# A decoder layer in fp32r: the context's M and U computed for two heads at once, and new places for the late steps

## The chip, the cores and the metric

One core of a Trainium2 chip. The metric is device microseconds of one execution. The engines are TensorE (PE, the matrix engine, whose weight loads are shown as PEld), VectorE (DVE), ScalarE (ACT), GpSimd (POOL) and SyncE (SP, which issues most DMAs). Each engine works through its own list of instructions in order, and waits on semaphores where it needs another's result.

## The reference

A decoder layer on x of 2 x 1024 x 256 with a context of 2 x 77 x 256, 16 heads of 64 in both attentions:

```
x = layernorm(x + self_attention(x))              # causal, rotary positions
x = layernorm(x + cross_attention(x, context))
x = layernorm(x + routed_ffn(x))                  # only the 512 tokens with the highest router value

cross_attention(query, key=value=context):
    q = query @ w_q; k = key @ w_k; v = value @ w_v       # split into heads
    attn = softmax(q @ k.T / 8)
    return (attn @ v) @ w_o
```

## The kernel before

Every large operand stands as a rounded high half and a low half (the difference), and a product is three matmuls: high by high, high by low, low by high. ACT writes the high half, POOL or DVE the low one.

One function, `plan()`, makes a single ordered list of steps, and each engine runs its own part of every step in that order. A step has a due time, counted in score steps, from hand-written tables; the steps are sorted by it. A step is named by a key and numbers, as sc.126 or kt.3. So the tables decide the order on every engine's queue at once, SP's and POOL's too.

*Self-attention.* Sixteen passes, one for a pair of heads and one batch entry (`NSELF`), with nine score steps each: sc.0 to sc.143. In sc, PE computes a block of scores for the two heads of the pair, one on rows 0 to 63 of the array and one on rows 64 to 127, alternating (line 682). Each has its own PSUM bank; ACT takes the exponentials (line 942). mx is a run of matmuls for the row maxima, with reductions on DVE. pv (line 701) is the product with V, four to a pass. su adds the exponentials, on POOL and some on DVE (line 504). sm sums over keys (line 713), den and nrm turn and spread the reciprocals, op is a piece of the output projection. Of the next passes pj, vp and st are projected and rounded in between.

*The context.* Instead of K and V of the context, the kernel makes for each head M = w_q k' (so that the scores are x times M) and U = v w_o (so that the output is a sum of P times U). For each pair p of heads, eight in all:

- xw.p.0 and xw.p.1: the pair's weights. SP has loaded them into one of two buffers (`load_xw`, line 1621); ACT rounds them, POOL makes the low half (lines 888 and 1451), and SP issues the load of the next pair's half when POOL is done.
- kt.p: `context_kv`, twelve matmuls with 128 rows for keys and values of both heads; ACT and DVE write their halves `XKH`, `XKL`.
- mh.h: `head_m`, M of one head, six matmuls on the 64 rows of that head. ACT copies it out in two pieces (line 1006), DVE makes three low pieces (lines 1278 and 1282).
- uh.h: `head_u`, U of one head, six matmuls of 77 by 256 on the same 64 rows. ACT copies it out, and SP stores it to `ud` in HBM (`keep_u`, line 1671).
- ug.k: U comes back from `ud` in another layout, ten pieces: load (line 1637), ACT, POOL. The load of ug.k+2 waits until POOL is done with ug.k (two buffers). wg are the same for the weights of the feed-forward part.
- tx.2.k turns x for the cross-attention.

PE takes PSUM banks from rings: kt, mh, uh, mx, sm, den, nrm, op and pj share five banks ("self"), taken in turn; `take` waits until the bank's last user has been copied out.

All these steps, keyed by `ENDS`, fall into the last two passes, from sc.126 on. Of pair p, xw, kt, mh and uh come at a fixed offset from `kt + by * p`.

*The rest.* sx.u (scores, 16 tiles of 128 queries), the maxima and exponentials, dn.u (sums on DVE, division on POOL), tp.u (turns) and pu.u (times U); keyed by `TAIL`. lns and lnr are the two halves of a layer norm: statistics on DVE and roots on POOL (line 1499), and rows scaled on DVE (line 1259). lw, lg, ct, sl, ps, id, gt route the tokens, xg turns the chosen ones. h1, fin, fl are the feed-forward part, keyed by `FFN`, and po (`put_rows`, line 1575) scatters the finished rows to the output.

## Time and profile before

| | us |
|---|---|
| median of 3 runs | 923.16 (920.53 to 923.82) |
| the profiled execution | 924.77 |
| its span, first to last instruction | 922.9 |
| PE busy in it | 839.0 (91%) |
| DVE busy | 698.5 (76%) |
| POOL busy | 650.0 (70%) |
| ACT busy | 446.0 (48%) |
| mean granted clock of PE | 0.959 |

Busy time is the union of an engine's instructions. An engine can be busy for all of a stretch and still not be what sets it, so the table of stretches is read together with what each wait names. [...] In PE's timeline matmuls overlap: one starts before the one ahead of it has ended, and the time from start to start is its real cost.

### The profile page before, as it was taken

The numbers are of one execution on the slowest core, as the hardware profiler recorded it, in microseconds if no ns is written. First come the engines' busy times: TensorE is split into PE (matmuls) and PEld (weight loads), VectorE is DVE, ScalarE is ACT, GpSimd is POOL, SyncE is SP. The second block draws the span as 40 slices with busy tenths as digits, with TensorE's granted clock in tenths as the row PEclk, the third lists the DMA queues.
The fourth block names the chain that finished last, engine by engine and source line by source line (L and its number), as shares of the span: only waits on it lengthen the run. The fifth ranks groups of instructions, "written<-read, shape, count | busy, mean of one in ns | idle before, by whom it ended". The sixth has DMA issues, their size and how long they took to land.

```text
span 922.9 us, 17631 instructions
## 1 busy us (share of the span) xinstructions
PE 839.0 (91%) x6322; PEld 625.5 (68%) x6322; DVE 698.5 (76%) x1722; ACT 446.0 (48%) x1009; POOL 650.0 (70%) x636
## 2 busy tenths in 40 slices
PE   2677999999998999999999999999998989878794
PEld 2554666766666667666666676677668979777594
DVE  3678777877879878788898797553359888998674
ACT  2323445455355453553544534655665754553450
POOL 2538697887977979889889898667566432453576
PEclk9879999999999999999999999999999989888798
DMA  8010000000001000000000010333111000120012
GB/s 267 24 58 12 8 24 8 18 25 7 19 1 30 14 7 30 13 8 25 11 14 1 8 36 1 94 90 93 55 44 34 24 24 25 43 71 24 23 47 91
DMA packets 33206, 33.47 MB, mean 36 GB/s; under 512 B 3616, under 2 KB 28000, under 8 KB 33120
## 3 DMA queue, kind: packets, MB, share of 16 engines
q1 hardware_dynamic: 32352, 30.26, 10.8%
q0 software_dynamic: 768, 2.10, 0.7%
q8 instruction: 50, 0.82, 0.4%
q14 instruction: 36, 0.29, 0.1%
HBM read 24.45 MB, written 7.77 MB: 35 GB/s over the span
## 4 chain that ended last, share of the span: by engine, by line
PE 69%; DVE 12%; POOL 6%; issue 6%; ACT 4%; DMA 1%; SPq 1%; DVEq 0%; POOLq 0%; ACTq 0%
PE bank L609 28%; PE bank L682 15%; PE bank L701 13%; PE bank L649 5%; PE bank L614 3%; ACT W_f L1048 2%; PE bank L713 2%; POOL SUM L504 1%; DVE X L1259 1%; DVE W_f L1366 1%; DVE DR L1366 1%; PE bank L687 1%; POOL out L1575 1%; POOL rs L1499 1%; POOL REG L1451 1%
## 5 line engine op out<-in xcount | busy, mean ns | idle before, releaser
L504 POOL TENSOR_TENSOR SUM<-SUM,PT_f 128x512 f32<-128x512 f32 (+3 forms) x272 | 254.4, 961 | 53.6 <-PE bank L701 50.8
L942 ACT ACTIVATE PT_f<-bank 128x512 f32<-128x512 f32 x224 | 121.5, 594 | 128.0 <-PE bank L687 89.2
L682 PE MATMUL bank<-REG 64*128 64x512 f32 (+3 forms) x1152 | 151.2, 361 | 2.5 <-DMA MR<-MH 2.4
L1185 DVE CUSTOM_DVE_ANT_0 bank<-bank,later 128x128 f32<-128x128 f32 (+3 forms) x256 | 118.2, 519 | 8.0 <-PE bank L649 7.9
L682 PEld LDWEIGHTS bank<-REG 64*128 64x128 f32 x1152 | 100.2, 188 | 34.8 <-issue 13.5
L1188 DVE TENSOR_REDUCE NM<-bank 128x1 f32<-128x512 f32 x128 | 82.2, 684 | 47.5 <-PE bank L649 47.5
L1451 POOL TENSOR_TENSOR REG<-RW_f,REG 128x512 fp32r<-128x512 f32 x64 | 83.1, 1306 | 38.6 <-ACT REG L888 38.5
L609 PE MATMUL bank<-XH,W_r 128*128 128x512 f32 x256 | 93.4, 418 | 17.6 <-POOL W_r L1451 17.6
L701 PE MATMUL bank<-PT_f,VV_f 128*64 128x512 f32 (+3 forms) x640 | 109.4, 471 | 0.0
L1476 POOL TENSOR_TENSOR RW_f<-RW_f,sinS 128x512 f32<-128x512 f32 x64 | 83.8, 1311 | 24.3 <-DVE RW_f L1157 24.2
L1451 POOL TENSOR_TENSOR W_r<-W_f,W_r 128x512 fp32r<-128x512 f32 (+1 forms) x56 | 64.6, 1157 | 35.4 <-ACT W_r L888 35.4
L649 PE MATMUL bank<-REG 64*128 64x512 f32 (+3 forms) x384 | 72.8, 413 | 10.7 <-DVE NM L1185 4.1
L1516 POOL TENSOR_TENSOR W_f<-W_f,RDEN 128x1232 f32<-128x1232 f32 x16 | 36.0, 2252 | 64.2 <-DVE RDEN L1304 64.2
L701 PEld LDWEIGHTS bank<-PT_f,VV_f 128*64 128x64 f32 x640 | 42.2, 137 | 55.5 <-issue 52.2
L1048 ACT ACTIVATE W_f<-bank,NM 128x77 f32<-128x77 f32 x256 | 56.8, 372 | 46.4 <-DVE NM L1294 46.4
L609 PEld LDWEIGHTS bank<-XH,W_r 128*128 128x128 f32 x256 | 50.1, 196 | 31.5 <-POOL W_r L1451 17.8
L682 PE MATMUL bank<-MR,oneR 64*128 64x512 f32 (+3 forms) x384 | 71.0, 345 | 0.0
L649 PEld LDWEIGHTS bank<-REG 64*128 64x128 f32 x384 | 35.0, 188 | 50.1 <-issue 36.5
L504 DVE TENSOR_TENSOR SUM<-SUM,PT_f 128x512 f32<-128x512 f32 (+1 forms) x48 | 59.2, 1233 | 10.9 <-POOL SUM L504 10.8
L888 ACT ACTIVATE REG<-RW_f 128x512 fp32r<-128x512 f32 x64 | 40.3, 629 | 40.9 <-DVE RW_f L1170 40.9
L942 ACT ACTIVATE SUM<-bank 128x512 f32<-128x512 f32 x64 | 34.5, 592 | 42.7 <-PE bank L687 42.4
L609 PE MATMUL bank<-XL,W_r 128*128 128x512 f32 x128 | 52.2, 408 | 0.0
(205 smaller groups left out, 2033.0 us busy)
## 6 DMA issues: line engine op xcount, KB each, us to landing
W_f<-in_cw SPq DMA_DIRECT2D x16, 256.0 KB, 2.7
W_f<-in_Wq SPq DMA_DIRECT2D x16, 128.0 KB, 2.5
W_f<-in_Wk SPq DMA_DIRECT2D x16, 128.0 KB, 2.8
XR_f<-in_xT SPq DMA_DIRECT2D x8, 256.0 KB, 4.1
W_f<-in_Wv SPq DMA_DIRECT2D x8, 256.0 KB, 3.0
W_f<-in_Wo SPq DMA_DIRECT2D x16, 128.0 KB, 2.3
...
W_f<-ud SPq DMA_DIRECT2D x8, 256.0 KB, 2.7
```

The costliest lines, as they stand in the source:

```text
L504: e.e.tensor_tensor(s, s, p_at(gp, c, kt, par), ALU.add).then_inc({"g": g_sum, "v": v_sum}[on], 1)
L609: i = e.matmul(o, a, b_, start=start and n == 0, stop=stop and n == len(terms) - 1)
L649: i = e.matmul(bank_of["mx", gp, j, par][:, o:o + w], op_at(gp, 0)[rows, 128 * qt:128 * qt + 128], op_at(gp, 2)[rows, 512 * kc:512 * kc + ...
L682: i = e.matmul(ST[par][:, o:o + w], keys[rows, :], qs[rows, q0:q0 + w], start=k == 0, stop=k == 3 and not diag)
L701: i = e.matmul(OB[rows, 512 - tile_width(c, kt):512], VV[vb][:, kt, col + 64 * par:col + 64 * par + 64], p_at(gp, c, kt, par), start=kt == ...
L888: return e.activation(o, i, ACT.Copy)
L942: e.activation(o[:, :], ST[par][:, :], ACT.Exp, scale=D ** -0.5).then_inc(a_exp, 1)
L1048: i = e.activation(P[u % 3][:, L * h:L * h + L], bank_of["sx", u, j][:, L * (h - h0):L * (h - h0) + L], ACT.Exp, bias=NM[u % 2][:, h:h + 1 ...
L1185: e.tensor_tensor_reduce(s, s, later[:, 512 - w:512], -1.0, -NEG, ALU.add, ALU.min, NM[gp % 2][:, col:col + 1]).then_inc(v_mr, 1)
L1188: e.tensor_reduce(NM[gp % 2][:, col:col + 1], s, AX.X, ALU.max, negate=True).then_inc(v_mr, 1)
L1451: return e.tensor_tensor(o, raw, hi.bitcast(F), ALU.subtract)
L1476: e.tensor_tensor(SH[j][:, :], SH[j][:, :], sinS[:, halves(c)], ALU.mult).then_inc(g_sin, 1)
```

## The change

1. `head_m` and `head_u` become `heads_m` and `heads_u`: a step is a pair p, not a head. It takes two banks, and the six matmuls of the one head alternate with the six of the other. One signal, by two, comes at the end. ACT, DVE and SP do in such a step what they did in two.
2. `heads_ready` reads a place of its own for every xw, kt, m and u (`x0` to `u7`), where before one offset served all pairs.
3. `TAIL` and `FFN` have other numbers in some places.

The order of the steps from sc.127 on, before:

```
sc.127 mx.15.2 xw.0.1 kt.0 xw.1.0 sm.13 xw.1.1 sc.128 mh.0 wrb uh.0 den.13 uh.1 kt.1 xw.2.0 mx.15.3
mh.1 xw.2.1 sc.129 mx.15.4 mh.2 uh.2 pv.56 su mx.15.5 su su uh.3 kt.2 xw.3.0 sc.130 mh.3 xw.3.1 nrm.13.0 ...
pv.57 mx.15.7 su.14.1.1 mh.6 uh.6 uh.7 sc.132 kt.4 xw.5.0 op.13.0 op.13.1 mh.7 ... uh.13 kt.7 mh.13 sc.136
mh.14 uh.14 uh.15 sm.14 mh.15 sc.137 den.14 sc.138 pv.60 su.15.0.1 su.15.0.3 su.15.0.2 ug.0 sc.139 nrm.14.0
su.15.1.6 nrm.14.1 ug.1 tx.2.0 sc.140 pv.61 su.15.1.1 tx.2.1 ug.2 sc.141 op.14.0 op.14.1 tx.2.2 su.15.1.2
sc.142 tx.2.3 ug.3 su.15.1.3 pv.62 su.15.1.4 sc.143 op.14.2 op.14.3 ug.4 su.15.1.5 pv.63 su.15.1.7 ...
```

and after:

```
sc.127 mx.15.2 xw.0.1 sm.13 sc.128 kt.0 xw.1.0 wrb xw.1.1 den.13 mx.15.3 sc.129 mx.15.4 uh.0 kt.1 mh.0 xw.2.0
pv.56 xw.2.1 su su mx.15.5 mh.1 uh.1 sc.130 nrm.13.0 kt.2 xw.3.0 xw.3.1 su nrm.13.1 ... sc.131 pv.57 uh.2
mx.15.7 mh.2 xw.4.0 su.14.1.1 kt.3 xw.4.1 sc.132 op.13.0 op.13.1 uh.3 kt.4 xw.5.0 mh.3 ... mh.6 uh.6 kt.7 sc.136
sm.14 uh.7 sc.137 mh.7 den.14 ug.0 sc.138 tx.2.0 pv.60 su.15.0.1 su.15.0.3 su.15.0.2 ug.1 tx.2.1 sc.139
nrm.14.0 ug.2 tx.2.2 su.15.1.6 nrm.14.1 sc.140 ug.3 pv.61 tx.2.3 su.15.1.1 sc.141 ug.4 op.14.0 op.14.1
su.15.1.2 sc.142 su.15.1.3 pv.62 su.15.1.4 sc.143 op.14.2 op.14.3 su.15.1.5 pv.63 su.15.1.7 ...
```

Behind sc.143, on DVE dn.1 comes ahead of op.15, lns.6 ahead of pu.0, tx.3.2, tx.3.3 and sx.15 earlier, ct.0.3 behind sx.13; in the feed-forward part lns.17, lns.20 to 23 and h1.1.3, h1.1.4 and h1.1.7 come earlier, fin.0.0 ahead of xg.1. On POOL the roots of lns.29, 30 and 31 each come ahead of the scatter that they followed: before lns.28 po.1.0 lns.29 po.1.1 lns.30 po.1.2 lns.31 po.1.3, after lns.28 lns.29 po.1.0 lns.30 po.1.1 lns.31 po.1.2 po.1.3.

The diff, with the tables cut:

```diff
-ENDS = {"ctx": -10, "xw0": 0.01, "xw1": 0.28, "m0": 0.62, "txby": 0.7, "u0": 0.82, "u1": 1.08, "ugby": 1.1,
-        "by": 1.13, "m1": 1.4, "kt": 1.52, "wrb": 2.2, "ug": 12.8, "tx": 13.95}
...
+ENDS = {"ctx": -10.02, "txby": 0.7, "ugby": 0.795414, "x0": 0.918057, "y0": 1.21806, "k0": 2.03146, "x1": 2.06222,
+        "wrb": 2.2, "y1": 2.36222, "u0": 3.08146, "k1": 3.17563, "m0": 3.2, "x2": 3.20639, "y2": 3.50639, "m1": 3.72,
...
+        "ug": 11.9543, "tx": 12.2954}
@@ heads_ready
-    for p in range(8):
-        o = at["kt"] + at["by"] * p
-        out += [(o, ("kt", p))]
-        o -= at["by"] if p else 0.6
-        out += [(o + at["xw0"], ("xw", p, 0)), (o + at["xw1"], ("xw", p, 1))]
-        o = at["kt"] + at["by"] * p
-        out += [(o + at[f"m{j}"], ("mh", 2 * p + j)) for j in range(2)]
-        out += [(o + at[f"u{j}"], ("uh", 2 * p + j)) for j in range(2)]
+    for p in range(NP):
+        out += [(at[f"x{p}"], ("xw", p, 0)), (at[f"y{p}"], ("xw", p, 1)), (at[f"k{p}"], ("kt", p)),
+                (at[f"m{p}"], ("mh", p)), (at[f"u{p}"], ("uh", p))]
@@ PE
-            def head_m(h):
-                p, par = divmod(h, 2)
-                i, rows = p % 2, slice(64 * par, 64 * par + 64)
+            def heads_m(p):
+                i = p % 2
                 pe.wait_ge(g_xw, 2 * p + 2)
                 pe.wait_ge(v_kt, p + 1)
-                bk = take(("mh", h), v_mh2, 3 * h + 3)
-                kh, kl = XKH[i][rows, 0:L2], XKL[i][rows, 0:L2]
+                bks = [take(("mh", 2 * p + par), v_mh2, 3 * (2 * p + par) + 3) for par in range(2)]
                 for n in range(2):
-                    wh, wl = (w[rows, 512 + 128 * n:640 + 128 * n] for w in (XWH[i], XWL[i]))
-                    j = mm(bk[:, L2 * n:L2 * n + L2], [(wh, kh), (wh, kl), (wl, kh)])
-                j.then_inc(p_mh, 1)
+                    for k in range(3):
+                        for par, rows in enumerate(HEAD):
+                            w = (XWH, XWH, XWL)[k][i][rows, 512 + 128 * n:640 + 128 * n]
+                            j = e.matmul(bks[par][:, L2 * n:L2 * n + L2], w, (XKH, XKL, XKH)[k][i][rows, 0:L2],
+                                         start=k == 0, stop=k == 2)
+                j.then_inc(p_mh, 2)
...
+            def heads_u(p):
+                i = p % 2
                 pe.wait_ge(g_xw, 2 * p + 2)
                 pe.wait_ge(v_kt, p + 1)
+                bks = [take(("uh", 2 * p + par), a_uh, 2 * p + par + 1) for par in range(2)]
                 for b in range(NB):
+                    for k in range(3):
+                        for par, rows in enumerate(HEAD):
+                            v = (XKH, XKH, XKL)[k][i][rows, L2 + L * b:L2 + L * b + L]
+                            w = (XWH, XWL, XWH)[k][i][rows, 768:1024]
+                            j = e.matmul(bks[par][0:L, 256 * b:256 * b + 256], v, w, start=k == 0, stop=k == 2)
+                j.then_inc(p_uh, 2)
@@ ACT (take_m, take_u) and DVE (lower_m) alike; SP:
-            def keep_u(h):
-                sp.wait_ge(a_uh, h + 1)
-                e.dma_start(ud[:, L * h:L * h + L, :].rearrange("b k c -> k b c"),
-                            USTG[h % 2][0:L, :].rearrange("p (b c) -> p b c", b=NB)).then_inc(d_ud[h % 2], 16)
-                if h == NH - 1:
+            def keep_u(p):
+                for h in (2 * p, 2 * p + 1):
+                    sp.wait_ge(a_uh, h + 1)
+                    e.dma_start(ud[:, L * h:L * h + L, :].rearrange("b k c -> k b c"),
+                                USTG[h % 2][0:L, :].rearrange("p (b c) -> p b c", b=NB)).then_inc(d_ud[h % 2], 16)
+                if p == NP - 1:
                     load_staged(0)
                     load_staged(1)
```

## Rows read from the trace of the kernel before

**Rows 1.** The page's chain that ended last: share of the span by engine

```profile
PE 69%; DVE 12%; POOL 6%; issue 6%; ACT 4%; DMA 1%; SPq 1%; DVEq 0%; POOLq 0%; ACTq 0%
```

**Rows 2.** Table of stretches: us, length, busy us of engines, PEclk granted clock, DMA

```profile
578.20:637.90 59.70, 55.62 (x474) 43.45 (x474) 30.22 (x90) 37.03 (x86) 40.45 (x38) 0.97 0.36 104
585.80:590.40 4.60, 4.60 (x32) 2.70 (x34) 0.48 (x1) 2.03 (x4) 2.34 (x2) 0.63 0.38 114
637.20:641.60 4.40, 4.09 (x23) 2.84 (x24) 2.13 (x8) 2.68 (x9) 4.13 (x4) 0.61 0.05 15
657.00:682.10 25.10, 23.72 (x163) 15.19 (x163) 12.14 (x16) 15.43 (x37) 25.05 (x29) 1.00 0.16 47
700.00:820.00 120.00, 111.01 (x782) 106.17 (x781) 109.03 (x271) 68.87 (x260) 54.23 (x48) 0.94 0.12 37
```

**Rows 3.** Timeline (start, us, what, idle before), all engines, 583 to 592

```profile
583.24 1.07 ACT L942 ACTIVATE PT_f<-bank 128x512 f32<-128x512 f32 x2
...
584.40 2.49 POOL L1451 TENSOR_TENSOR W_r<-W_f,W_r 128x512 fp32r<-128x512 f32 x2
...
585.76 0.31 PE L609 MATMUL bank<-CH,W_r 128*128 128x154 f32 x1 [2.27 <-issue]
...
587.42 1.94 PE L713 MATMUL bank<-SUM,ones 128*32 128x512 f32 x8
...
591.04 0.87 PE L609 MATMUL bank<-RW_r,W_r 64*128 64x154 f32 x6
```

**Rows 4.** Timeline of PE, 647.9 to 650.3

```profile
648.01 1.17 PE L609 MATMUL bank<-W_r,RW_r 64*77 64x256 f32 x12
649.12 1.06 PE L713 MATMUL bank<-SUM,ones 128*32 128x512 f32 x8
```

**Rows 5.** Groups of PE by line and form, 590.9 to 651.5

```profile
L609 PE MATMUL bank<-RW_r,W_r 64*128 64x154 f32 x96 | 13.3, 278 | 0.3 <-issue 0.3
```

**Rows 6.** Timeline of PE, 634 to 642

```profile
633.99 0.92 PE L609 MATMUL bank<-W_r,RW_r 64*77 64x256 f32 x6
...
637.54 0.64 PE L609 MATMUL bank<-RW_r,W_r 64*128 64x154 f32 x4 [0.31 <-issue]
```

**Rows 7.** Timeline of PE in an early pair, 106.9 to 108.4

```profile
107.79 0.60 PE L682 MATMUL bank<-REG 64*128 64x256 f32 x6
```

**Rows 8.** Timeline of PE, 616 to 623.9

```profile
618.79 0.34 PE L609 MATMUL bank<-CH,W_r 128*128 128x154 f32 x1 [1.49 <-POOL W_r L1451]
...
621.74 1.19 PE L609 MATMUL bank<-RW_r,W_r 64*128 64x154 f32 x12
```

**Rows 9.** Groups of ACT by line, 590 to 652: busy, mean ns, idle before

```profile
L1006 ACT ACTIVATE REG<-bank 128x154 fp32r<-128x154 f32 x16 | 4.8, 299 | 4.8 <-PE bank L609 4.7
L888 ACT ACTIVATE cosS<-bank 77x512 f32<-77x512 f32 x8 | 4.8, 594 | 0.7 <-PE bank L609 0.7
```

**Rows 10.** Groups of DVE by line, the same stretch

```profile
L1278 DVE SCALAR_TENSOR_TENSOR XR_r<-bank,REG 128x154 fp32r<-128x154 f32 x16 | 5.1, 318 | 14.8 <-ACT VV_r L1006 14.8
```

**Rows 11.** Timeline of POOL, 636 to 683

```profile
657.05 4.20 POOL L504 TENSOR_TENSOR SUM<-SUM,PT_f 128x384 f32<-128x384 f32 x6 [14.29 <-PE bank L701]
```

**Rows 12.** Timeline of SP's queue (issues of DMAs), 642 to 683

```profile
650.20 0.28 SPq L1671 DMA_DIRECT2D ud<-sinS  x1
652.81 15.83 SPq L1637 DMA_DIRECT2D W_f<-ud  x4
```

**Rows 13.** The page's DMA issues: count, KB each, us to landing

```profile
W_f<-ud SPq DMA_DIRECT2D x8, 256.0 KB, 2.7
```

**Rows 14.** Timeline of POOL, 903 to 923

```profile
910.29 1.08 POOL L1575 DMA_INDIRECT out<-SUM,rows  x1 [0.74 <-DVE SUM L1259]
...
911.72 0.57 POOL L1499 TENSOR_TENSOR rs<-rs,half 128x1 f32<-128x1 f32 x1
...
918.54 1.09 POOL L1575 DMA_INDIRECT out<-SUM,rows  x1 [0.74 <-DVE SUM L1259]
```

**Rows 15.** Timeline of DVE, 684 to 700

```profile
694.64 2.73 DVE L1224 TENSOR_TENSOR X<-X,bank 128x512 f32<-128x512 f32 x4 [1.99 <-PE bank L609]
```

More of the change, by code:

```diff
@@ L46 @@
         "u1": 8.9}
-ENDS = {"ctx": -10, "xw0": 0.01, "xw1": 0.28, "m0": 0.62, "txby": 0.7, "u0": 0.82, "u1": 1.08, "ugby": 1.1,
-        "by": 1.13, "m1": 1.4, "kt": 1.52, "wrb": 2.2, "ug": 12.8, "tx": 13.95}
-TAIL = {"sm": -1.82, "den": -1.81, "n": -0.44, "o": 0.04, "dn": 0.2, "l1by": 0.21, "xgby": 0.3, "x3by": 0.3,
[7 rows of a table removed]
-FFN = {"s15": -0.6, "lw2": -0.5, "st7": -0.45, "r15": -0.3, "lw3": -0.2, "h0": 0, "xgby": 0.01, "ls0": 0.1,
[5 rows of a table removed]
+ENDS = {"ctx": -10.02, "txby": 0.7, "ugby": 0.795414, "x0": 0.918057, "y0": 1.21806, "k0": 2.03146, "x1": 2.06222,
[6 rows of a table added]
+TAIL = {"sm": -1.82, "den": -1.81, "n": -0.44, "dn": 0.2, "l1by": 0.21, "o": 0.21, "x3by": 0.3, "xgby": 0.31,
[7 rows of a table added]
+FFN = {"s15": -0.6, "st7": -0.45, "a9": -0.44, "r15": -0.3, "lw2": -0.21, "lw3": -0.2, "h0": 0, "xgby": 0.01,
[5 rows of a table added]
 GROUPS = [(0, 4), (4, 6), (6, 7), (7, 8)]
@@ L876, in _ @@
                     "xg": turn_chosen, "h1": hidden,
-                    "fin": second, "fl": second_low, "put": lambda *k: give("turn", *k), "ad": lambda *k: give("pj", *k), "kt": context_kv, "mh": head_m, "uh": head_u, "sx": scores_x,
+                    "fin": second, "fl": second_low, "put": lambda *k: give("turn", *k), "ad": lambda *k: give("pj", *k), "kt": context_kv, "mh": heads_m, "uh": heads_u, "sx": scores_x,
                     "tp": turn_p, "pu": p_u}
@@ L998, in take_kv, with take_m, take_m1 @@
                 copy(XKH[p % 2], bank_of["kt", p][:, 0:2 * L2]).then_inc(a_kt, 1)
-            def take_m(h):
+            def take_m(p):
+                for h in (2 * p, 2 * p + 1):
+                    take_m1(h)
+            def take_m1(h):
                 ac.wait_ge(p_mh, h + 1)
@@ L1007, in take_m, with take_u, take_u1 @@
                                  scale=D ** -0.5).then_inc(a_mh, 1)
-            def take_u(h):
+            def take_u(p):
+                for h in (2 * p, 2 * p + 1):
+                    take_u1(h)
+            def take_u1(h):
                 ac.wait_ge(p_uh, h + 1)
@@ L1270, in lower_kv, with lower_m, lower_m1 @@
                                 ALU.subtract).then_inc(v_kt, 1)
-            def lower_m(h):
+            def lower_m(p):
+                for h in (2 * p, 2 * p + 1):
+                    lower_m1(h)
+            def lower_m1(h):
                 m = bank_of["mh", h][:, 0:2 * L2].rearrange("p (k b n) -> p k b n", k=2, b=2)
@@ L1667, in next_xw @@
                     load_xw(p + 1, i)
-            def keep_u(h):
-                sp.wait_ge(a_uh, h + 1)
-                e.dma_start(ud[:, L * h:L * h + L, :].rearrange("b k c -> k b c"),
-                            USTG[h % 2][0:L, :].rearrange("p (b c) -> p b c", b=NB)).then_inc(d_ud[h % 2], 16)
-                if h == NH - 1:
+            def keep_u(p):
+                for h in (2 * p, 2 * p + 1):
+                    sp.wait_ge(a_uh, h + 1)
+                    e.dma_start(ud[:, L * h:L * h + L, :].rearrange("b k c -> k b c"),
+                                USTG[h % 2][0:L, :].rearrange("p (b c) -> p b c", b=NB)).then_inc(d_ud[h % 2], 16)
+                if p == NP - 1:
                     load_staged(0)
```

8 lines of the change are left out of this document (removed), and 26 rows, old and new, of tables (ENDS, FFN, TAIL).

## The prediction

> **What bounds the kernel now.** I read first the chain of work that ended last [rows 1]: TensorE (PE) holds 69% of it, VectorE (DVE) 12%, GpSimd (POOL) 6%. Then the table of stretches [rows 2], because the change touches one stage mainly. In that table the last-but-one self-attention pair (578.2 to 637.9, score steps 126 to 134, into which most of the context's work is woven) takes 59.7 us, with PE busy 55.6 of them: PE sets this stage. Then comes the last pair (to 682.1), where from 657.0 to 682.1 POOL is busy 25.05 of 25.10: POOL sets that stretch. From 700 to 820 DVE is busy 109 of 120, so the cross-attention is DVE's. Last I read the waits inside each stretch, engine by engine, from [rows 3] on.
>
> Steps are called by their names in the plan: kt.p (keys and values of the context for pair p), mh and uh (M and U, before for a head, after for a pair), sc.n (score step), pv, sm, ug, as in the code.
>
> **Part 1, where the first pieces stand.** Before, PE comes to kt.0 at 583.5 and waits 2.27 us, until POOL has made the low half of its weights (584.40, two halves of 1.25) [rows 3]. Behind the wait the granted clock is 0.63 on average from 585.8 to 590.4 [rows 2], so sm.13 takes 1.94 there where sm.14's eight take 1.06 at full clock [rows 4], and sc.128 1.75 instead of 1.4. After, sm.13 and sc.128 stand ahead of kt.0 on PE. Both are ready (sc.127's exponentials run from 583.24 and end at 584.3 [rows 3]) and fill 583.5 to 585.9 at full clock; kt.0 then finds its weights at 585.7. kt.0 ends at 587.3, when before all three were done at 591.0. Gain 3.7 us: 2.3 of wait, 1.4 of clock. If POOL were later, the wait would come back for just that time; nothing queued on POOL ahead of this weight changes.
>
> **Part 2, two heads side by side.** It removes no matmul. M is 96 matmuls on 64 rows of the array, 154 columns, 278 ns each and pipelined [rows 5]; U is 96 of 256 columns, as long. A block of six occupies PE from its start to the next one's start 0.71 us (M, 591.04 to 591.75) [rows 3] or 0.85 (U, 633.99, with 0.07 of its 0.92 beside the next) [rows 6]. After, the six of one head alternate with six of the other half of the array. What the trace shows of such pairs is a score step with 256 columns: six matmuls, three pairs, in 0.60 from first start to last end [rows 7], starts of a pair 1 to 4 ns apart and pairs 117 ns apart, which is a single block's own pace. So I take 0.76 for a block of twelve, M or U. Sixteen single blocks of M and sixteen of U would be 25 us, but they already share the array in part: where a block of the other half or a score step follows, that starts early (two M blocks, twelve matmuls, 1.19 to the end of the last, of which some 0.16 lie beside the next block, so 1.03 instead of 1.42) [rows 8]. Read block by block on PE's timeline, from the first at 591.04 [rows 3] to the last two, which begin at 648.01 [rows 4], the 31 blocks take 19.3 us from start to next start. Fifteen pairs there take 11.5. Gain 7.8. Bounds: 0 if halves exclude each other, 12 if nothing was shared before.
>
> **Part 3, waits in the middle.** At 617.3 PE waits 1.49 for kt.4's weights [rows 8]: POOL's queue has an add of the probabilities ahead, which waits for pv.57. After, kt.3 and sc.132, the two op pieces and uh.3 stand between pv.57 and kt.4, 6.5 us of PE work, while POOL needs 1.4 + 1.3 + 1.3 + 1.5 = 5.5 to reach that weight. The wait goes. At 637.2 PE waits 0.31 [rows 6], and the clock is 0.61 on average to 641.6 [rows 2], half speed for 3.4 us, worth 1.7. I take that as gone with its wait. Together 3.5; bounds 1.5 and 4.1. I also walked the weight path for each pair (load 2.7, ScalarE's (ACT's) rounding 0.6, POOL's difference 1.3, the next load behind that): kt.5, kt.6 and kt.7 then have margins of about 3, 2 and 2 us. POOL has 26 us of work from pv.57 to the last weight, PE 27 to kt.7: close, and the next thing to be late.
>
> **Part 4, what a pair adds.** A pair takes two banks of the ring of five at once, and one signal at its end frees neither earlier. Behind its last matmul (0.27) stand, for M, ACT's two copies of 0.3 per head (starts 0.19 apart, 0.38 in all) and DVE's differences of 0.5 per head, for U two copies of 0.6 in turn [rows 9, 10]. The second bank is free 1.6 us (M) or 1.35 (U) after. Walking the plan I find one clear collision (uh.2, a mx step, mh.2: 0.5 us), and small ones behind it. What queues behind such a wait on PE is the next score step, and ACT's exponentials wait for that. The trace has no wait of this kind by itself, so I bound it: 0, to 0.5 at each of 16 placements, 8 us. I take 2, since most placements have kt, pv or scores between them. SP issues a pair's two stores (0.28 each) behind one wait instead of two; the weight loads behind them have the margins of part 3. The count of changes between 64-row and 128-row work on PE stays 46 in these two stages.
>
> The row first: in this kernel the copies out of the banks for M and U are 16 x (0.38 + 0.6) = 16 us of ACT in a stretch where ACT idles over a third. [...]
>
> At sc.137 this makes 3.7 + 7.8 + 3.5 - 2 = 13.0.
>
> **Part 5, the last pair.** The gain must pass POOL. Before, POOL is idle 14.29 us until pv.60, then has one block to 682.05, 25.0 us, with all five ug pieces in it [rows 11]. After, ug.0 stands first. From the last U's end (649.2) the trace goes: last store issued 650.20, first load of ud 652.81 [rows 12], landing 2.7 [rows 13], 0.6 on ACT: 7.0 us. After, uh.7 ends at 637.6, so POOL starts at 644.6, not 657.05. pv.60, which the adds need, ends by about 644. The same 25.0 of work then ends at 669.6: 12.5 of the 13.0 arrive. Moved with ug: ACT waits for each landing with sc.138's, 140's, 141's and 142's exponentials behind it. The fetch of ug n+2 follows POOL's split of ug n, 2.7 + 0.6. On POOL's list at least 4 us of other work lies between, so it is hidden; PE stands still some 2 us for an op piece, with as much slack before sm.15.
>
> **Part 6, the end and the tail.** After PE's last matmul the end is a ping-pong: root (0.9), rows scaled on DVE, scatter issued (1.08), 2.75 us for each of four pieces, 910.29 to 918.54 [rows 14]. After, each root stands ahead of the scatter before it, so DVE scales while POOL issues. From 908.6: two roots 1.8, scatter 1.2, root 0.9, 1.1, 0.9, 1.1 and 1.1, the last start is near 916.4. Gain 2.1, bounds 1 and 3. In the cross-attention one move has a row: DVE waits 1.99 for op.15 at 692.6 and does the next tile's sums behind them [rows 15]; after, the sums stand in the gap. Of the other moves (ct.0.3 later, sx.15, tx.3.2, lns.6, lns.17 and lns.20 to 23 earlier, lone weight pieces, fin.0.0 before xg.1) none removes work. I take 1.4 for the lot, bounds -3 and +5, for DVE has 11 us idle in 120 there.
>
> **The sum.** 12.5 + 2.1 + 1.4 = 16.0. The profiled execution took 924.77 (span 922.9, 1.9 around it): 908.8. The median of the runs, 923.16, is 1.6 below it: 907.2, forecast 907.
>
> **Rivals.**
> Evictions take part of it: 0.5 us at each placement, 8 instead of 2: 913. For it: the signal at the end of the pair. Against: five banks, and PE's waits in this stretch today name no copy.
> Slower than before: each of 16 placements waits for a full release with one score step's exponentials ahead on ACT (1.4 to 1.6, and 1.08, so 2.5): 40 instead of 2, 945. The change breaks even at 1.1 us a placement, 18 in all. Against: kt's 1.4 or more lies between most.
> The fetches of ud show: two of five round trips (4.6 each: split, load, rounding) uncovered, 9.2: 916. For it: ACT's order; against: POOL's list.
> The halves don't overlap for these shapes: 7.8 and the 3 that blocks shared are lost: 918. Against: the pairs of [rows 7].
> The tail's moves are worth 5 more than I give: DVE's idle time is there to be filled; below 902.
>
> **Chances.** Forecast 0.62 (902 to 911), evictions 0.13, fetches 0.08, halves 0.03, slower 0.04, the tail 0.10. The range 900 to 916 leaves out about two in ten. About 0.5% (4.6 us) is what a measurement here can tell from no change: faster than 918.5 is 0.89, within 0.5% 0.07, slower 0.04.
>
> **What would show it.** PE from sc.126 to sc.135 near 46 us instead of 59.7, without the clock's two falls; M's and U's starts in pairs some 4 ns apart; kt.0 still at about 585.8 but sc.128 ahead of it; POOL's last block, 25 us, starting near 644.6; sm.15 12 to 13 us sooner than 682; scatters at the end 1.9 to 2.1 apart. It would be wrong if PE's waits name ACT's or DVE's copies behind the pairs, if POOL has gaps between 645 and 670, or if the time between sm.15 and the end (240 us) changes by more than 5.

## The result, and the profile after

The changed kernel takes 916.48 us (median of 13 runs, 911.1 to 920.8), the kernel before, measured beside it, 922.92 (13 runs, 920.4 to 927.2): ratio 0.9928, 95% interval 0.9902 to 0.9953. Measured again, it took 915.18 (6 runs; before beside it 922.58), 0.9894 (0.9851 to 0.9938). Forecast were 907 and a range of 900 to 916: the sign is right, the gain is 6.4 us (7.4 the second time) where 16 was forecast.

The 19 runs of the changed kernel aren't spread evenly: their spans are 909.3 to 912.6 in seven and 914.4 to 918.9 in twelve. The mean granted clock is 0.962 to 0.968 in the seven and 0.956 to 0.962 in the twelve. The profiled execution of the first 13 is one of the seven (912.28 us, span 910.5), so its trace shows the change nearly as forecast up to the last pair. The second profile (e1, span 914.4) is one of the twelve, and shows what is missing. Both are read here.

Stretches of the changed kernel (columns as in [rows 2]): from sc.126 to sc.135, where kt.0 stands, and 120 us of the cross-attention.

```profile
577.20:627.30 50.10, 47.47 (x472) 35.66 (x472) 32.24 (x87) 34.47 (x81) 40.29 (x38) 1.00 0.39 112
584.80:589.40 4.60, 4.37 (x46) 3.70 (x42) 2.50 (x9) 2.82 (x6) 2.33 (x2) 1.00 0.42 114
690.00:810.00 120.00, 106.40 (x737) 101.49 (x736) 103.97 (x257) 67.44 (x252) 52.24 (x46) 0.95 0.12 37
```

The first stage takes 50.1 us instead of 59.7, and the clock stays at its upper level (PEclk 1.00), where [rows 2] has 0.63 behind kt.0. (The prediction's sign of "near 46 us" for this stage doesn't follow from its own parts, of which some stand behind sc.135, the clock's fall at 637 among them.) Now PE's timeline around kt.0, answering [rows 3]:

```profile
584.05 0.60 PE L682 MATMUL bank<-REG 64*128 64x256 f32 x6
...
584.79 0.33 PE L609 MATMUL bank<-CH,W_r 128*128 128x154 f32 x1
...
588.29 0.88 PE L814 MATMUL bank<-W_r,RW_r 64*77 64x256 f32 x12
...
591.01 0.90 PE L799 MATMUL bank<-RW_r,W_r 64*128 64x154 f32 x12
```

sc.128 ends ahead of kt.0 (584.79), which waits for nothing. A pair's U (588.29) and M (591.01) are groups of twelve; their matmuls of different halves start 3 to 4 ns apart at first. From a block's first start to the next step's it is 0.83 for this M (591.01 to 591.84). Read so over all sixteen blocks on PE's timeline, they take 0.72 to 0.88 each, 12.6 us in sum, 0.79 on average.

GpSimd, answering [rows 11], and the scatters, answering [rows 14]:

```profile
644.14 1.27 POOL L1467 TENSOR_TENSOR REG<-W_f,REG 128x512 fp32r<-128x512 f32 x1 [5.12 <-ACT REG L892]
645.38 4.20 POOL L504 TENSOR_TENSOR SUM<-SUM,PT_f 128x384 f32<-128x384 f32 x6
...
660.47 8.82 POOL L504 TENSOR_TENSOR SUM<-SUM,PT_f 128x512 f32<-128x512 f32 x8 [0.69 <-DVE SUM L504]
669.25 0.73 POOL L1467 TENSOR_TENSOR W_r<-W_f,W_r 128x256 fp32r<-128x256 f32 x1
```

```profile
899.54 0.59 POOL L1515 TENSOR_TENSOR rs<-rs,half 128x1 f32<-128x1 f32 x1
900.31 1.07 POOL L1591 DMA_INDIRECT out<-SUM,rows  x1 [0.18 <-issue]
...
902.56 1.08 POOL L1591 DMA_INDIRECT out<-SUM,rows  x1 [0.19 <-issue]
...
904.76 1.20 POOL L1591 DMA_INDIRECT out<-SUM,rows  x1 [0.19 <-issue]
906.26 0.98 POOL L1591 DMA_INDIRECT out<-SUM,rows  x1 [0.30 <-issue]
```

GpSimd begins ug.0 at 644.14 (forecast 644.6) and ends its sums at 669.29 (forecast 669.6), with one gap of 0.69. But this execution starts sc.126 1.0 us sooner than the one before did, so counted from there both are 0.5 and 0.7 later than forecast. The roots stand ahead of the scatters, which start 2.25, 2.20 and 1.50 us apart instead of 2.75.

What PE waited for from sc.126 to nrm.15.1, in the kernel before and in the two profiles of the changed kernel (us in total, times, longest). The first profile has one line more, 0.2 for a reduction of VectorE; of the second the first two of eight lines are shown, the others are the first profile's within 0.2:

```profile
PE bank L609 <- issue: 2.6, 2, 2.3
PE bank L609 <- POOL W_r L1451: 1.5, 1, 1.5
PE bank L713 <- POOL SUM L504: 1.4, 1, 1.4
PE bank L614 <- ACT DR L888: 0.7, 1, 0.7
```

```profile
PE bank L614 <- ACT DR L892: 1.9, 1, 1.9
PE bank L814 <- issue: 1.5, 1, 1.5
PE bank L682 <- ACT SUM L946: 0.7, 1, 0.7
PE bank L799 <- ACT cosS L892: 0.6, 1, 0.6
PE bank L713 <- POOL SUM L504: 0.5, 1, 0.5
PE bank L682 <- ACT PT_f L946: 0.4, 1, 0.4
PE bank L609 <- POOL W_r L1467: 0.4, 1, 0.4
...
```

```profile
PE bank L814 <- issue: 2.3, 1, 2.3
PE bank L614 <- ACT DR L892: 1.9, 1, 1.9
...
```

The waits of before for weights (2.3 and 1.5) are gone; 0.4 are left, ahead of kt.1. A new one stands ahead of uh.3: 1.5 in the one, 2.3 in the other, "issue" since the profile names no releaser for it. VectorE, GpSimd and PE around it in the second:

```profile
607.32 4.37 DVE L504 TENSOR_TENSOR SUM<-SUM,PT_f 128x512 f32<-128x512 f32 x1
611.61 0.47 DVE L1281 TENSOR_TENSOR RW_r<-bank,RW_r 128x308 fp32r<-128x308 f32 x1
```

```profile
606.14 1.28 POOL L1467 TENSOR_TENSOR NU_r<-NU_f,OH 128x512 fp32r<-128x512 f32 x1
607.39 1.28 POOL L1467 TENSOR_TENSOR W_r<-W_f,W_r 128x512 fp32r<-128x512 f32 x1
608.63 1.29 POOL L504 TENSOR_TENSOR SUM<-SUM,PT_f 128x512 f32<-128x512 f32 x1
609.88 1.26 POOL L1467 TENSOR_TENSOR W_r<-W_f,W_r 128x512 fp32r<-128x512 f32 x1
```

```profile
612.18 0.93 PE L814 MATMUL bank<-W_r,RW_r 64*77 64x256 f32 x12 [2.30 <-issue]
...
615.79 1.56 PE L799 MATMUL bank<-RW_r,W_r 64*128 64x154 f32 x12
```

```profile
613.00:620.00 7.00, 7.00 (x42) 5.83 (x42) 2.64 (x11) 3.66 (x10) 3.08 (x3) 0.51 0.27 78
```

uh.3 needs the low half of kt.3 (L1281). This stands in VectorE's queue behind one add of the probabilities (L504, su.14.1.1), and the add takes 4.37 us, until 0.55 after the end of GpSimd's run of instructions, which start 1.25 us apart. PE stands still for 2.30 us, and then the granted clock is 0.51 on average from 613 to 620, the lower level (0.50) for 6.8 us of it: the same M block takes 1.56 where it took about 0.9. In the first profile the add took 3.55, the wait was 1.48, and the clock stayed up.

The end of the last pair hangs on another chain. Followed back from den.15 in the first profile (start, us, what), it runs from the last U through its store, the fetch of ug.0 and GpSimd, and then:

```profile
655.35 4.98 DVE SUM L504
...
664.64 1.31 POOL SUM L504
...
666.05 1.47 DVE SUM L504
...
668.19 1.01 ACT W_f L1060 x5
...
671.76 0.49 ACT DR L892
```

GpSimd waits for a second long add of VectorE (su.15.1.1). One of its own adds then releases VectorE's last add; behind this stand the maxima of sx.0, behind them sx.0's sixteen exponentials on ScalarE (3.56 us), and behind these, in ScalarE's queue, the copy DR that den.15 needs.

Start of some steps after that of sc.126, in us, read from PE's timelines. The first column is sc.126's own start (the time ahead of it is the same program in all and differs by 2.8 us at most; of it the clock was at its lower level for 20.5 us in the quickest and 27.3 in the slowest), the last are den.15 to the first gather, how much of that the granted clock was at its lower level, and the gather to the end.

| profile | at | sc.129 | sc.137 | pv.63 | den.15 | nrm.15.1 | to gather | at lower clock | to end |
|---|---|---|---|---|---|---|---|---|---|
| before | 578.2 | 17.8 | 72.2 | 95.7 | 105.7 | 110.0 | 132.9 | 13.7 | 106.1 |
| after | 577.2 | 9.9 | 59.4 | 84.8 | 95.1 | 99.4 | 134.4 | 9.7 | 103.8 |
| e1, after again | 577.0 | 9.9 | 63.2 | 88.6 | 98.9 | 103.2 | 134.9 | 13.3 | 103.7 |
| e2, tail's tables old | 578.5 | 9.9 | 63.5 | 88.8 | 99.2 | 103.5 | 133.3 | 13.7 | 106.1 |
| e3, tail's tables only | 578.1 | 17.8 | 70.7 | 94.1 | 104.2 | 108.5 | 133.5 | 6.2 | 103.9 |
| e4, not in turns | 579.0 | 9.9 | 60.7 | 86.2 | 96.3 | 102.2 | 134.0 | 9.8 | 103.8 |
| e5, add behind | 576.9 | 9.9 | 58.7 | 83.9 | 93.9 | 98.2 | 134.6 | 15.4 | 102.1 |
| e6, kt.0 first | 577.0 | 15.4 | 62.9 | 88.2 | 98.6 | 102.9 | 134.8 | 13.5 | 103.6 |
| e7, pairs, old places | 578.7 | 17.0 | 66.7 | 89.9 | 99.8 | 104.1 | 132.2 | 10.2 | 106.4 |
| e8, old feed-forward | 578.6 | 9.9 | 62.7 | 87.9 | 98.3 | 103.9 | 135.9 | 16.4 | 106.4 |
| e9, e5 and old cross | 578.1 | 9.9 | 58.7 | 83.9 | 94.3 | 100.1 | 133.8 | 13.5 | 103.1 |
| e10, e5 not in turns | 577.4 | 9.9 | 60.8 | 86.4 | 96.7 | 101.0 | 133.3 | 9.9 | 103.7 |
| e11, e5, ug.0 later | 577.9 | 9.9 | 58.7 | 83.5 | 94.5 | 100.2 | 136.1 | 16.6 | 103.5 |
| e12, one operand | 577.3 | 9.9 | 57.9 | 83.2 | 93.5 | 99.4 | 136.5 | 19.8 | 103.9 |
| e13, two such | 576.2 | 9.9 | 57.6 | 83.1 | 92.7 | 98.6 | 136.2 | 19.3 | 103.4 |

From den.15 to nrm.15.1 it is 4.3 us in nine profiles and 5.6 to 5.9 in six (e4, e8, e9, e11, e12, e13). In these six the clock fell to its lower level for 3.4 us near the end of the wait of 1.9 ahead of den.15 or up to 1.4 us behind it; this wait is in all twelve profiles with the new places of the context's steps (before, e3 and e7 have 0.7). In e12, from den.15 on:

```profile
670.80:676.70 5.90, 5.85 (x27) 5.34 (x28) 1.78 (x4) 2.96 (x10) 0.00 (x0) 0.71 0.00 0
```

So differences at nrm.15.1 are compared within one of the two groups, or at den.15.

### The profile page after: what moved, and what is told of

Its sections match the earlier page's. It is cut to its first block, busy times and chain, and to the rows that moved or that the text cites. A ratio compares the mean times of both kernels' runs of the same rounds, so it can differ in the third digit from the quotient of the medians.

```text
span 910.5 us, 17643 instructions
## 1 busy us (share of the span) xinstructions
PE 829.5 (91%) x6322; PEld 616.6 (68%) x6322; DVE 704.7 (77%) x1722; ACT 444.5 (49%) x1009; POOL 650.0 (71%) x636
## 4 chain that ended last, share of the span: by engine, by line
PE 66%; DVE 12%; POOL 7%; issue 6%; ACT 5%; DMA 2%; SPq 1%; DVEq 0%; POOLq 0%; ACTq 0%
PE bank L609 26%; PE bank L682 14%; PE bank L701 12%; PE bank L649 5%; ACT W_f L1060 3%; PE bank L614 3%; POOL SUM L504 2%; PE bank L713 2%; POOL REG L1467 1%; PE bank L837 1%; DVE X L1271 1%; DVE X L1241 1%; POOL out L1591 1%; DVE W_f L1382 1%; DVE SUM L504 1%
## 5 line engine op out<-in xcount | busy, mean ns | idle before, releaser
L504 POOL TENSOR_TENSOR SUM<-SUM,PT_f 128x512 f32<-128x512 f32 (+3 forms) x272 | 255.7, 965 | 33.4 <-PE bank L701 29.6
L682 PE MATMUL bank<-REG 64*128 64x512 f32 (+3 forms) x1152 | 148.1, 359 | 4.1 <-DMA MR<-MH 3.0
L682 PEld LDWEIGHTS bank<-REG 64*128 64x128 f32 x1152 | 97.3, 187 | 35.8 <-ACT PT_f L946 14.0
L1467 POOL TENSOR_TENSOR REG<-RW_f,REG 128x512 fp32r<-128x512 f32 x64 | 83.2, 1307 | 38.0 <-ACT REG L892 37.9
L649 PE MATMUL bank<-REG 64*128 64x512 f32 (+3 forms) x384 | 71.8, 411 | 10.7 <-DVE NM L1197 4.6
L504 DVE TENSOR_TENSOR SUM<-SUM,PT_f 128x512 f32<-128x512 f32 (+1 forms) x48 | 65.2, 1359 | 6.3 <-POOL SUM L504 6.2
L682 PE MATMUL bank<-MR,oneR 64*128 64x512 f32 (+3 forms) x384 | 68.1, 343 | 0.0
L649 PEld LDWEIGHTS bank<-REG 64*128 64x128 f32 x384 | 34.4, 187 | 49.4 <-issue 36.6
```

The lines of the kernel that those rows point to most:

```text
L504: e.e.tensor_tensor(s, s, p_at(gp, c, kt, par), ALU.add).then_inc({"g": g_sum, "v": v_sum}[on], 1)
L649: i = e.matmul(bank_of["mx", gp, j, par][:, o:o + w], op_at(gp, 0)[rows, 128 * qt:128 * qt + 128], op_at(gp, 2)[rows, 512 * kc:512 * kc + ...
L682: i = e.matmul(ST[par][:, o:o + w], keys[rows, :], qs[rows, q0:q0 + w], start=k == 0, stop=k == 3 and not diag)
L1467: return e.tensor_tensor(o, raw, hi.bitcast(F), ALU.subtract)
```

## The experiments

**The first four.** At this point two accounts stood against each other: the context's stage had kept its gain and the tail took it back, or the stage's gain itself varies. e1 is the changed kernel once more.

> The changed kernel itself, for a second profile and for how its executions scatter (911.1 to 920.8 in the first 13, before 920.4 to 927.2). Theory A, the cross-attention and what follows take back some 6 us in most executions while the context keeps its gain: sc.137 again 12 to 14 us sooner than in before, and the time from the start of nrm.15.1 to the end (234.7 us in before, 233.9 in the first profile) 236 to 242 in an execution of 916 or more. Theory B, the gain of the context itself varies from execution to execution: sc.137 only 6 to 9 us sooner in a slower one, and the rest unchanged at 234.

915.18 us, 0.9894 (0.9851 to 0.9938). Its stage takes 103.2 us where the first profile's took 99.4: the gain in the stage varies, and the rows above say where.

**e2** is the changed kernel with the two tables of the tail (`TAIL` and `FFN`) as before, **e3** the kernel before with the changed ones only (the diff is e3's, e2 takes it back).

```diff
-TAIL = {"sm": -1.82, "den": -1.81, "n": -0.44, "o": 0.04, "dn": 0.2, "l1by": 0.21, "xgby": 0.3, "x3by": 0.3,
+TAIL = {"sm": -1.82, "den": -1.81, "n": -0.44, "dn": 0.2, "l1by": 0.21, "o": 0.21, "x3by": 0.3, "xgby": 0.31,
...
-FFN = {"s15": -0.6, "lw2": -0.5, "st7": -0.45, "r15": -0.3, "lw3": -0.2, "h0": 0, "xgby": 0.01, "ls0": 0.1,
+FFN = {"s15": -0.6, "st7": -0.45, "a9": -0.44, "r15": -0.3, "lw2": -0.21, "lw3": -0.2, "h0": 0, "xgby": 0.01,
...
```

> The changed kernel with the tables TAIL and FFN of before: pairs and the new places of the context's pieces alone. Theory A1, the moves in TAIL and FFN are what costs: the whole 12.5 us arrive, median 910 to 911 (ratio 0.986). Theory A2, the moves are worth the 3.5 us forecast and arriving earlier costs by itself: slower than the changed kernel, 918 to 920. Theory B: about 919, as the context's gain is only 6 and the moves' 3.5 are missing.

> The kernel before with only the tables TAIL and FFN of the changed one. Theory A1 (the moves cost): slower than before by 3 to 6 us, 926 to 929. Theory A2 and theory B (the moves are worth what was forecast, 2.1 at the end and 1.4 in the rest): 919.5. In both the last four scatters start 1.9 to 2.2 us apart instead of 2.75.

e2: 917.22 (8 runs, 912.4 to 919.0), 0.9906 (0.9872 to 0.994). e3: 921.50 (12 runs), 0.9982 (0.9959 to 1.0006). The tail's tables alone bring 1.1 us, not told from nothing, where 3.5 was forecast; and the changed kernel without them (e2) is 0.7 to 2.0 slower than with them. None of the three figures expected of e2 is met. e2's profile has the long add too (4.47 us) and a stage of 103.5.

**e4** doesn't take turns: the six matmuls of one head, then the other's six, in the same blocks.

```diff
-                for n in range(2):
-                    for k in range(3):
-                        for par, rows in enumerate(HEAD):
+                for par, rows in enumerate(HEAD):
+                    for n in range(2):
+                        for k in range(3):
...
```

> The changed kernel, but in each step of M and U the six matmuls of one head come before the six of the other; banks, signals and places stay. It measures the pairing alone. Forecast: sc.137 7 to 8 us later than in the changed kernel (0.76 us a block of twelve becomes 1.3 or so), and the median up by as much, about 924. Rival, the pairing is hidden behind the weight path or the evictions: under 3 us.

913.39 (6 runs), 0.9889 (0.985 to 0.9927), no slower than with turns; the forecast of 924 falls, and the rival (under 3 us) stands. But in e4's profile the add at 610.6 took 1.67 us and nothing waited ahead of uh.3, so two things differ. e10 takes them apart.

**The next four.** **e5** moves the add.

```diff
-        items += [(p, ("su", gp, *t)) for p, t in zip(adds, CHAIN)]
+        items += [(5.75 if (gp, t) == (NSELF - 2, (1, 1)) else p, ("su", gp, *t)) for p, t in zip(adds, CHAIN)]
```

> The changed kernel with one step moved: the sums' add of group 14's piece (1,1), which stands in VectorE's queue ahead of the difference for kt.3, comes behind it (kt.3 and the add change places in the plan; nothing else moves). [...] With the add behind, the difference for kt.3 starts at about 608.0, the wait ahead of uh.3 is under 0.4 us, there is no fall of the clock between 600 and 640, nrm.15.1 starts 99 to 100.5 us after sc.126 (99.4 without the fall, 103.2 and 103.5 with it), and the median is 2 to 4 us under that of the changed kernel, 912 to 913.5. Theory B (the wait only shows an engine that is behind anyway): another wait takes its place before sc.137 and the median stays at 915 to 917.

912.19 (6 runs, 909.3 to 913.3), 0.9887 (0.9869 to 0.9904). VectorE in e5:

```profile
607.81 0.48 DVE L1281 TENSOR_TENSOR RW_r<-bank,RW_r 128x308 fp32r<-128x308 f32 x1 [0.30 <-issue]
608.20 3.52 DVE L504 TENSOR_TENSOR SUM<-SUM,PT_f 128x512 f32<-128x512 f32 x1
```

The add still takes 3.52 us, but the difference for kt.3 is ahead of it, the wait before uh.3 is gone, the clock stays up, and the stage takes 98.2. All six runs, and the twelve of e9 to e11 which have this order too, have spans of 907.5 to 912.1: the group at 914 to 919, with twelve of 19 runs of the changed kernel, is no longer there. The forecast of 912 to 913.5 is met and theory B falls; nrm.15.1 starts 98.2 after sc.126, sooner than forecast. e5 is 3.0 to 4.3 us faster than the changed kernel by the medians (the intervals of the ratios touch; it is the missing group that tells).

**e6** puts kt.0 ahead of sm.13 and sc.128 again, as it was.

```diff
-"k0": 2.03146
+"k0": 1.52
```

> The changed kernel with only the first piece put back: kt.0 again ahead of sm.13 and sc.128 (place 1.52 instead of 2.03). Theory A (Part 1 of the prediction): the wait for XWH[0] of 2.3 us ahead of kt.0 comes back, so kt.0 starts at about 585 us and sc.129 at 590.7 instead of 588.4 after the same start, and the clock falls to half for 3.4 us after it: 3 to 4 us longer, 918.5 to 920. Theory B (the wait moves into slack that other waits give back, since in the pairs version VectorE and GpSimd are the later ones): under 1 us, 915 to 917.

916.50 (12 runs), 0.9945 (0.9919 to 0.9971). PE in its profile:

```profile
584.58 0.31 PE L609 MATMUL bank<-CH,W_r 128*128 128x154 f32 x1 [2.27 <-issue]
...
586.64 1.94 PE L713 MATMUL bank<-SUM,ones 128*32 128x512 f32 x8
```

The wait of 2.27 us is back, as in [rows 3], with the clock's fall behind it; sc.129 is 5.5 us later, nrm.15.1 3.5 later than in the first profile of after, which has its own wait ahead of uh.3, and 4.7 later than in e5. By the median it is only 0 to 1.3 us slower than the changed kernel, which looks like theory B; but the shift also moved the add to 612.55, where it took 1.68 us. Against e5, where the add does no harm either, it is 4.3 slower. So theory A holds for what the wait costs, once like is compared with like; its median of 918.5 to 920 isn't met, for it left out that the later add isn't long.

**e7** is the kernel before with two heads to a block, M at the place of the second head's M and U at that of the second's U.

```diff
-        out += [(o + at[f"m{j}"], ("mh", 2 * p + j)) for j in range(2)]
-        out += [(o + at[f"u{j}"], ("uh", 2 * p + j)) for j in range(2)]
+        out += [(o + at["m1"], ("mh", p)), (o + at["u1"], ("uh", p))]
```

> The kernel before with the heads' M and U computed two at a time (M at the place of the second head's M, U at the place of the second head's U), and all places otherwise as before. Theory A (Part 2 of the prediction: what counts is that the blocks of two heads lie side by side): the stage from sc.126 to nrm.15.1 takes 7 to 8 us less than before's 110.0, some of it given back to waits since U now stands late in each pair's span, 916 to 918. Theory B (the gain is in the places, which fit the waits, and not in the pairing): under 3 us, 920 to 923.

919.04 (8 runs), 0.9957 (0.9942 to 0.9972): 3.9 faster than before, between the two theories. At sc.137 it is 5.5 ahead, at nrm.15.1 5.9, with both waits for weights still there (2.3 and 2.4 us). Up to sc.137 PE waits 5.6 in all (0.6 for ScalarE's copy and 0.3 for VectorE among it), where it waited 4.1 before, so the pairs by themselves give about 7.0.

**e8** has before's table for the feed-forward only.

> The changed kernel with the places of the feed-forward stage of before and the new ones of the cross-attention. Theory A (Part 6 of the prediction): the scatters at the end are 3.3 us apart again instead of 2.2 and the end comes 2.1 us later, 917 to 918.5. Theory B (the end goes by TensorE's last pieces, so the scatters' gain is what was late in the cross-attention): under 0.7 us, 915 to 917.

920.91 (12 runs), 0.9962 (0.9941 to 0.9983), 4 to 6 slower than the changed kernel and 3.7 slower than e2, which has both tables old. From the first gather to the end the four profiles with the old table take 106.1 to 106.4, those with the new one 102.1 to 103.9: the scatters' 2.3 are shown. (From PE's last matmul to the end it is 12.2 to 12.3 in these four and 9.4 in all the others.) Of the 4.7 us between the profiles of e8 and e1, 2.7 stand there, 1.6 ahead of sc.126, where both run the same program, and 1.0 between den.15 and the gather, where e8 has 3.1 us more at the lower clock (up to den.15 e8 is 0.6 ahead). e8 and e2 differ in the cross-attention's table alone, and e8, with the new one, is 3.7 slower in the median: the new places there cost something, or at least bring nothing.

**Three more, all with e5's order.** **e9** adds before's table of the cross-attention, **e10** takes no turns (e4's edit), **e11** has ug.0 behind sc.138 (and with it, by the same number, ug.3 and ug.4 behind sc.140 and sc.141):

```diff
-"ug": 11.9543
+"ug": 12.01
```

> The kernel with the add behind kt.3 (e5), and the cross-attention's places of before (the feed-forward's stay the new ones). Theory A (the cross-attention's moves cost): from nrm.15.1 to the first gather it took 128.6 us in before, 129.1 with both tables old, and 130.1 to 130.6 in five of the profiles with the new places; so this run needs 129, and the median is 1 to 1.5 us under e5's 912.2, about 911. Theory B (the tables fit each other only together, as the run with only the feed-forward's places old showed, 920.9 against 917.2 with both old): longer than e5 by 2 us or more, 914 to 916.

> The kernel with the add behind kt.3 (e5), and the twelve matmuls of a block not in turns: the six of one head, then the six of the other. [...] Theory B (Part 2 of the prediction, a block of twelve in turns takes 0.76 us and one that is not 1.2): 16 blocks of 0.2 to 0.4 us, 3 to 7 us longer, 915 to 919.

> The kernel with the add behind kt.3 (e5), and ug.0 right behind sc.138 instead of ahead of it. Theory A (ScalarE is held by ug.0's copy, which waits for its transfer, with the exponentials of sc.138 behind it: they start at 642.7 where sc.138 ended at 639.3): the exponentials start at about 641.0, TensorE's wait of 0.5 us ahead of sc.139 goes, and the end comes 0.4 to 0.9 us sooner, about 911.5. Theory B (the sums' chain on GpSimd and VectorE sets sm.15, where TensorE waits 0.2 us for GpSimd and 1.9 us for the copy of the sums): pv.63 sooner, den.15 not, and the median the same within 0.4 us.

e9: 911.87 (4 runs, as e10 and e11), 0.9879 (0.9862 to 0.9895), the same as e5, where theory A expected 1 to 1.5 us less and theory B 2 or more longer: between these two the cross-attention's moves bring nothing and cost nothing that can be told. In its profile the stretch to the gather is 0.8 shorter. e10: 913.19, 0.989 (0.9874 to 0.9907). PE in e10, the first blocks:

```profile
588.54 1.17 PE L814 MATMUL bank<-W_r,RW_r 64*77 64x256 f32 x12
...
591.25 1.19 PE L799 MATMUL bank<-RW_r,W_r 64*128 64x154 f32 x12
592.37 1.08 PE L701 MATMUL bank<-SUM,VV_f 128*64 128x512 f32 x4
```

The M block takes 1.12 us from its start to the next instead of 0.83, U 1.17 to its last end instead of 0.88, since the second head's six start beside the first's last ones but not beside its first ([rows 8] has the same 1.19 for two single blocks of M). The sixteen blocks take 16.0 us in sum instead of 12.6. At sc.137 e10 is 2.1 behind e5, at nrm.15.1 2.8, in the median 1.0, which the intervals don't tell from nothing. So taking turns is worth 2 to 3 us in the stage, not 7. Neither forecast holds as it stands: the median is near that of no difference (911.5 to 913), the stage nearer theory B. e4's good time was the missed wait. e11: 913.77, 0.9896 (0.9879 to 0.9912). ScalarE's exponentials of sc.138 start at 641.91, where e5's start at 642.74 although e5 is 1.0 us ahead there, and the wait ahead of sc.139 is gone; but VectorE's add at 654.1 then takes 6.24 us, PE waits 1.1 for GpSimd's sums, den.15 is 0.6 later than in e5 and the median 1.6 slower. Theory A falls, and theory B (the same median) holds no better; two more pieces moved with ug.0, so e11 doesn't show which of them costs.

**The last two.** Moving the add showed what its length costs, not why it is long. **e12** gives that one instruction a single operand in SBUF, leaving out one block of the sums of one group; **e13** does so for group 15 as well, and leaves out that block there too.

```diff
+                    if (gp, c, kt, on) == (NSELF - 2, 1, 1, "v"):
+                        e.e.tensor_reduce(s[:, 0:1], p_at(gp, c, kt, par), AX.X,
+                                          ALU.max).then_inc(v_sum, 1)
+                        continue
```

> The changed kernel, all in its places, with one instruction of VectorE replaced: group 14's add of piece (1,1) (SUM <- SUM, PT, two operands from SBUF) is a maximum over the same 512 columns of PT into one column of SUM (one operand from SBUF). It leaves out one block of the sums of one group's keys. [...]

> As the run with one operand, and group 15's add of piece (1,1) (654 us; 4.27 to 6.24 us in every profile of the changed kernel and of those made from it) replaced in the same way. It leaves out one block of the sums of two groups' keys. Theory A (that long add costs what the last pair gives back): it takes 0.7 us, pv.63 starts 24.0 us or less after sc.137 in place of 25.2 to 25.4 (before 23.5), and the median is 1 to 2 us under the run with one operand replaced. Theory B (the long add is covered: TensorE waits there for ScalarE's exponentials and for the copy of the sums): pv.63 25 us after sc.137, the same median within 0.5 us.

e12: 911.73 (6 runs), 0.9882 (0.986 to 0.9904). e13: 910.35 (6 runs), 0.9863 (0.984 to 0.9886). VectorE in e12 and GpSimd beside it:

```profile
607.82 0.68 DVE L505 TENSOR_REDUCE SUM<-PT_f 128x1 f32<-128x512 f32 x1
608.41 0.47 DVE L1285 TENSOR_TENSOR RW_r<-bank,RW_r 128x308 fp32r<-128x308 f32 x1
```

```profile
606.95 1.30 POOL L1471 TENSOR_TENSOR NU_r<-NU_f,OH 128x512 fp32r<-128x512 f32 x1
608.20 1.30 POOL L1471 TENSOR_TENSOR W_r<-W_f,W_r 128x512 fp32r<-128x512 f32 x1
609.44 1.30 POOL L508 TENSOR_TENSOR SUM<-SUM,PT_f 128x512 f32<-128x512 f32 x1
```

In the same place, with the same GpSimd work beside it and the same data to wait for, the instruction takes 0.68 us, no wait and no fall of the clock follow ahead of sc.137, and the median is that of e5; 911 to 913 was forecast for the case that the add is long by its two operands, 915 to 917 for the case that VectorE waited for data or its queue. So it was neither the data nor the queue: what was long as an add beside GpSimd's instructions is short as a reduction. The two differ in more than their operands (the reduction writes one column), but the traces hold a nearer control. VectorE in the first profile, 300 to 680, by shape:

```profile
L504 DVE TENSOR_TENSOR SUM<-SUM,PT_f 128x512 f32<-128x512 f32 x20 | 32.5, 1626 | 1.7 <-POOL SUM L504 1.6
L1236 DVE TENSOR_TENSOR X<-X,bank 128x512 f32<-128x512 f32 x40 | 26.3, 680 | 2.6 <-PE bank L609 2.4
```

The second is an add of the same size with one operand in PSUM. All 960 of them in the 15 profiles take 0.67 to 0.69 us, 936 beside a GpSimd tensor_tensor; those with both operands in SBUF take up to 6.24, see the last section. So among adds of this size only those with both operands in SBUF are long; the mechanism behind it isn't shown.

e13 is 1.4 us under e12, but not in the way its theory A said: pv.63 starts 25.5 after sc.137, as theory B had it, and the gain comes at sm.15 and den.15, where PE's wait for GpSimd's sums (0.4) is gone and den.15 starts 0.8 sooner. The intervals overlap, so the 1.4 is likely and not shown. (Its text says that this add is long in every profile made from the changed kernel; in e4 it took 1.17.)

## Why the prediction went wrong, step by step

**Part 1 (3.7 for the first pieces) was right.** Wait and fall of the clock are gone in every profile of the changed kernel; the three pieces are done 9.0 us after sc.126 instead of 12.8, 3.8 where 3.7 was forecast. Put back, wait and fall cost 4.7 at nrm.15.1 and 4.3 in the median (e6 against e5).

**Part 2 (7.8 for the pairs) was right.** Its 0.76 us for a block measured 0.79 on average, 15 blocks of 11.8 instead of 11.5: 7.5 beside its 19.3 for the single blocks. Pairs alone, in old places, give 5.5 at sc.137 with 1.5 more of waits than before (e7), so about 7.0. What they owe to the turns is 2.1 at sc.137 and 3.4 in the blocks (e10 against e5); the rest comes already from two blocks of different halves standing next to each other.

**Part 3 (3.5 for waits in the middle) was half of the story, and here is the step that failed.** kt.4's wait and the fall at 637 went as forecast. But the walk of "the weight path" went over SP, ScalarE and GpSimd, and not over VectorE, whose queue also stands between kt.3 and uh.3. In the kernel before this queue had slack; moved forward, its add of su.14.1.1 meets GpSimd in mid-run. The prediction put this at nothing. It costs 1.5 to 2.4 us of wait and, in three of four profiles (e1, e2, e8, not the first), 6.8 us at half clock behind it: 3.3 to 4.1 at sc.137 over the first profile (59.4 against 62.7 to 63.5), 4.0 to 4.8 over e5, and 3.0 to 4.3 in the median (e5). A smaller miss of the same walk is 0.4 us for kt.1's weights.

**Part 4 (2.0 for what a pair adds) was right in kind and more than twice too large.** The one collision that the plan's walk found is in the rows: PE's M waits 0.6 for ScalarE's copy. Together with 0.2 for VectorE it is 0.8; the first rival, 8 us of evictions, is refuted.

At sc.137 the first profile of after has 12.8 of the 13.0, and that is partly luck: 0.8 of these are M of pair 7, which stood ahead of sc.137 and now stands behind it, and the 1.2 that Part 4 put too high make up for most of the 1.5 and 0.4 of waits that nobody forecast. In e1, near the median, 9.0 arrive.

**Part 5 (12.5 of 13.0 arrive) was wrong by 2.** The last U ends where it was forecast, GpSimd starts 0.5 late and ends its sums 0.7 late (both from sc.126), so sm.15 comes 11.8 us sooner. The step that failed is to take the end of GpSimd's block for what sets den.15. The copy for den.15 stands in ScalarE's queue behind sx.0's sixteen exponentials, and these hang on a GpSimd add inside the block, the one that releases VectorE's last add. Before, the exponentials ended at 683.17 and sm.15 at 683.19, so it made no difference. After, all five pieces of ug stand ahead of that add (before, 1.7 us of them came behind), and GpSimd waits 0.7 for VectorE's second long add: the add's end is 10.4 sooner, and den.15 and nrm.15.1 are 10.6. That is read from the trace's chain; no run moved these steps. The long add's share is what e13 shows, 0.8 at den.15. PE itself waits 0.7 and 0.4 for ScalarE's exponentials behind the rounding of ug.0, which is why pv.63 has 10.9; I had named ScalarE's order and priced it at nothing. And in six of twelve profiles the clock falls at the wait ahead of den.15, which costs another 1.3 to 1.6.

**Part 6: the end (2.1) was right, 2.3 measured; the tail's moves (1.4) weren't.** (The steps that it adds up for the end give 916.7, not 916.4.) By the medians the moves in the cross-attention bring nothing: 911.87 without them and 912.19 with them (e9, e5), 917.22 and 920.91 (e2, e8). VectorE, which I expected to fill its 11 us of idle time, has 16 in the 120 us (104.0 busy instead of 109.0). From den.15 to the gather the profiles with the new places need 133.3 to 136.5, the four with the old ones 132.2 to 133.8. Much of the spread goes with the clock: those with the new places and under 10 us at the lower clock need 133.3 to 134.4, those with over 16 need 135.9 to 136.5. At 13.3 to 13.7 us of it the new ones take 134.9 and 134.8 (e1, e6) and the old ones 132.9, 133.3 and 133.8 (before, e2, e9), so 1 to 2 us are left that the moves seem to cost. Through which wait is open.

So e1's profile, near the median, accounts for the 16.0 as follows: den.15 is 6.8 sooner where 12.5 was forecast (3.8 of the gap are the long add with the clock's fall, 1.9 the last pair), the stretch to the gather is 2.0 longer instead of 1.4 shorter, and the end brings 2.4. That leaves 7.2. With the long add out of the way e5 stands at 912.2, 10.7 under before; what still lacks to 907 is the last pair and the tail. The best version run here is e5 (or e9, which can't be told from it); e12 and e13 leave work out.
